# Shared expert's later quarters placed between the routed experts, three experts rounded early instead of five, one ring of four result tiles

## The chip, the cores and the metric

One Trainium2 chip, all 8 cores. Each core takes one of the 8 sequences (batch element b on core b) and runs the same program with the same weights; the cores exchange nothing. The time of a run is the device time of the slowest core in microseconds. A result is given as the median of several runs, and one execution more is taken with the hardware profiler.

## What is computed

One layer, for x of 8 x 2048 x 1024 in float32. First x plus an RWKV attention of the layer-normed x, then that plus a feed-forward part of its layer norm. Cut to what matters here:

```
xk, xv, xr = mixes of ln(x) with its shift by one token
k, v, r = xk@Wk.T, xv@Wv.T, xr@Wr.T ; wkv = recurrence over the 2048 tokens
x = x + (sigmoid(r) * wkv) @ Wo.T
f = ln(x)
combine = top-2 of 16 softmax router weights      # expert 15 is the identity
routed = combine[:, 15] * f + sum over e < 15 of combine[:, e] * ((silu(f@G[e]) * (f@U[e])) @ D[e])
shared = (silu(conv3(f)) * (f@Us)) @ Ds           # conv3: causal, kernel of 3 tokens, 1024 -> 512
x = x + shared + routed
```

## The kernel before

The text below calls TensorE PE, VectorE DVE, ScalarE ACT, GpSimd POOL and SyncE SP. Every engine has its own program in an order written out by hand, and they meet by counting semaphores. POOL issues all DMAs that convert float32 to bfloat16, that add in DRAM, or that go by an index; they run in the software queue q0. SP issues the plain ones, in the hardware queue q1. Both queues use the same 16 DMA engines.

**Attention** (to about 385 us). The tokens go in 4 chunks s of 512. For each chunk, 8 units d of 128 channels make k, v and r (24 matmuls) and the recurrence (`wkv` on DVE). In the chunk after it, `wo_tile` multiplies by the output weights, `x1add` adds to x (`x1r`, two buffers, loaded from x and stored to out by SP: tile g+2 is loaded after tile g has been stored), and `ln2` normalizes. From unit 7 on, POOL issues two `precast` DMAs for each unit: they turn the weights of the experts in `PRE` into bfloat16 in DRAM (`ewb_d`), a half matrix each, 30 in all, up to unit 21.

**Shared expert.** `gate_up(("S", c), ic)` makes a quarter ic of the 512 channels for chunk c: 24 matmuls for the convolution and 8 for `su`. `base(g)` multiplies a tile of 128 tokens by `sd` (8 matmuls); DVE copies the result to `fx[g % 4]`, and POOL adds it to out (`add_base`). A two-token halo is copied on DVE (`halo_s`). Chunks 0 and 1 stand among the router's work (`top2`, `ranks`, `route`). When the last tokens are routed, POOL scatters the table of positions, loads it as `ti`, and gathers rows.

**Routed experts** (from about 577 us). 15 experts, 320 rows each (3 tiles). For expert e PE does gate_up quarters 0 and 1, `down(e - 1)`, quarter 2, `rows_in(e + 1)` (transposes of the gathered rows) and quarter 3. ACT and DVE scale the results of `down` into `ysb` (a ring of 5 tiles), and POOL adds them to rows of out by index (`add_rows`). Adds of one expert are issued only when those of the expert before have landed, since two of them may touch the same row. ACT's and DVE's `yout(e - 1)` stand between silu and product of quarters 1 and 2 of expert e, and wait there for a free tile. Weights are 3 matrices of 1 MB (bfloat16) for each expert in 9 slots: from float32 by POOL (`expert_w`), or for experts of `PRE` from `ewb_d` by SP (`pre_w`), each when its slot is free (`w_free`). Weights 0 to 8 (experts 0 to 2) need not wait for an expert.

POOL's order in the loop of experts is:

```
rows(e + 2)
if e: add_rows(e - 1); expert_w(3 * e + 8)
if e == 1: add_rows(NE)        # the identity expert
expert_w(3 * e + 9), expert_w(3 * e + 10)
```

Of the kernel before, what the change touches and what calls it, by code (L numbers as in the profile page):

```python
# [30 lines left out]
PRE = [3, 5, 7, 9, 11]  # L31
NPOS = 128 * NPC

# [14 lines left out]
def build_one(ms, rec):  # L48
# [93 lines left out]
    wsl += [place(f"wsl{6 + j}", [128, 4096], BF16, o_m1 + 8192 * j)[0] for j in range(3)]  # L142
# [7 lines left out]
    xgT = [place(f"xgT{j}", [128, CC, CAP], BF16, o_x1 + 5120 * j)[0] for j in range(3)]  # L150
# [4 lines left out]
    xrow = [place(f"xrow{j}", [128, C], BF16, (o_y + 8192 if j < 4 else o_lt - 8192) + 2048 * j)[0] for j in range(8)]  # L155
    lnS = [place(f"lnS{j}", [128, CC, 528], BF16, o)[0] for j, o in enumerate((o_x, o_t))]
    sg = [place(f"sg{j}", [128, 512], F32, o_t + 8448 + 2048 * j)[0] for j in range(2)]
    ysb = [place(f"ysb{j}", [128, C], F32, o_m0 + 4096 * j)[0] for j in range(5)]
    idr = [place(f"idr{j}", [128, C], BF16, o_x + 2048 * j)[0] for j in range(TT)]
    hE = [place(f"hE{j}", [128, ICC, CAP], BF16, o)[0] for j, o in enumerate((o_m0 + 20480, o_x + 8448))]  # L160
    fx = [place(f"fx{j}", [128, C], F32, o_b + 4096 * j)[0] for j in range(4)]
# [23 lines left out]
    with ExitStack() as st:  # L185
# [12 lines left out]
        s_xrow = [sem(f"s_xrow{i}") for i in range(8)]  # L198
# [6 lines left out]
        s_acc = [sem(f"s_acc{i}") for i in range(2)]  # L205
# [6 lines left out]
        blocks = [("S", q) for q in range(NCH)] + [("E", e) for e in range(NE)]  # L212
        gu = {}
        for b in blocks:
            for ic in range(ICC):
                gu[(b, ic)] = len(gu)

        order = [0, NE] + list(range(1, NE))

        def ytile(e, j):  # L220
            return order.index(e) * TT + j
# [4 lines left out]
        def w_free(m):  # L226

            p = m - 9
            if p % 3 == 2:
                return MS(f"t:d{ytile(p // 3, TT - 1)}_1")  # L230
            return MS(f"t:{'gu'[p % 3]}{gu[(('E', p // 3), ICC - 1)]}")

        def ysb_free(eng, q):
            if q >= 5:
                k = (q - 5) // TT
                eng.wait_ge(s_acc[k % 2], 16 * TT * (k // 2 + 1))
# [40 lines left out]
        def _(t):  # L277
# [117 lines left out]
            def rows_in(e):  # L395
                for j, (o, w) in enumerate(TOKTILES):
                    n = column(e, j)
                    t.wait_ge(s_xrow[n % 8], 16 * (n // 8 + 1))
# [6 lines left out]
                    for kc in range(CC):  # L405
                        mm = t.transpose(xgps(n)[:, kc, 0:w], xrow[n % 8][0:w, 128 * kc:128 * (kc + 1)], IDM[0:w, 0:w])  # L406
# [7 lines left out]
            def gate_up(b, ic):  # L414
# [10 lines left out]
                if kind == "S":  # L425
# [5 lines left out]
                    for kk in range(3):  # L431
                        for kc in range(CC):
                            mm = t.matmul(ps[:, pg, :], cwS[:, kk * CC + kc, osl],  # L433
                                          lnS[q % 2][:, kc, 14 + kk:526 + kk],
                                          start=(kk == 0 and kc == 0), stop=(kk == 2 and kc == CC - 1))
# [3 lines left out]
                    for kc in range(CC):  # L439
                        mm = t.matmul(ps[:, pu, :], suS[:, kc, osl], lnS[q % 2][:, kc, 16:528],  # L440
                                      start=(kc == 0), stop=(kc == CC - 1))
                    PE(mm, f"u{n}")
                else:
# [3 lines left out]
                    for j, (bank, key) in enumerate(((pg, "g"), (pu, "u"))):  # L447
# [3 lines left out]
                        for kc in range(CC):  # L451
                            mm = t.matmul(ps[:, bank, 0:CAP], slot_view(m)[:, kc, osl], xgT[q % 3][:, kc, :],  # L452
# [3 lines left out]
            def down(e):  # L456
# [3 lines left out]
                for j, (o, w) in enumerate(TOKTILES):  # L460
                    q = ytile(e, j)
                    for h in range(2):
                        if q == 0:
                            t.wait_ge(s_dv, MS(f"v:fa{NT - 1}"))
                        else:
                            p = ytile(e, j - 1) if j else ytile(e - 1, TT - 1)
                            if h == 0:
                                t.wait_ge(s_sc, MS(f"s:y{p}"))
                            else:
                                t.wait_ge(s_dv, MS(f"v:yo{p}"))  # L470
# [4 lines left out]
                        PE(mm, f"d{q}_{h}")  # L475

            def base(g):
                c, i = g // 4, g % 4
                if g == 0:
                    t.wait_ge(s_sd, 16)  # L480
                    t.wait_ge(s_dv, MS("v:x1_15"))
                else:
                    t.wait_ge(s_dv, MS(f"v:fa{g - 1}"))
# [42 lines left out]
            for c in range(2, NCH):  # L526
                for ic in range(ICC):
                    gate_up(("S", c), ic)
                    base(4 * (c - 1) + ic)
            for g in range(12, 16):  # L530
                base(g)
            rows_in(0)
            for e in range(NE):
# [7 lines left out]
                gate_up(("E", e), 3)  # L541
            down(NE - 1)

        @blk.vector
        def _(v):
# [158 lines left out]
            def xg_out(e):  # L704
                for j, (o, w) in enumerate(TOKTILES):
                    n = column(e, j)
                    if n % 2 == 1:
                        v.wait_ge(s_pe, MS(f"t:xt{n}"))
                        if e >= 3:
                            v.wait_ge(s_pe, MS(f"t:u{gu[(('E', e - 3), ICC - 1)]}"))  # L710
                        DV(v.tensor_copy(xgT[e % 3][:, :, o:o + w], xgps(n)[:, :, 0:w]), f"xg{n}")
                DV.ms[f"v:xgt{e}"] = DV.v

            def hmul(b, ic):
# [9 lines left out]
                else:  # L724
                    if ic == 0 and q >= 2:
                        v.wait_ge(s_pe, MS(f"t:d{ytile(q - 2, TT - 1)}_1"))
                    DV(v.tensor_tensor(hE[q % 2][:, ic, :], sg[n % 2][:, 0:CAP], ps[:, pu, 0:CAP], OP.mult), f"h{n}")  # L727

            def yout(e):
                for j, (o, w) in enumerate(TOKTILES):  # L730
                    q, n = ytile(e, j), column(e, j)
                    wgt = tiw[0:w, n, 1:2]
                    ysb_free(v, q)
                    if e < NE:
                        v.wait_ge(s_pe, MS(f"t:d{q}_1"))
                        DV(v.tensor_scalar(ysb[q % 5][0:w, 512:1024], ps[0:w, 7, :], wgt, None, OP.mult), f"yo{q}")  # L736
                    else:
                        v.wait_ge(s_idr[j], 16)
                        DV(v.tensor_scalar(ysb[q % 5][0:w, 512:1024], idr[j][0:w, 512:1024], wgt, None, OP.mult),
                           f"yo{q}")  # L740

            def halo_s(q):
                v.wait_ge(s_pe, MS(f"t:u{gu[(('S', q - 1), ICC - 1)]}"))
                v.wait_ge(s_ls[(q - 1) % 2], 16 * ((q - 1) // 2 + 1))
                DV(v.tensor_copy(lnS[q % 2][:, :, 14:16], lnS[(q - 1) % 2][:, :, 526:528]), f"halo_s{q}")  # L745

            def base(g):
                v.wait_ge(s_pe, MS(f"t:f{g}"))
                if g >= 4:
                    v.wait_ge(s_out[g % 4], 16 * (g // 4))  # L750
                DV(v.tensor_copy(fx[g % 4][:], ps[:, 6:8, :].rearrange("p a b -> p (a b)")), f"fa{g}")
# [16 lines left out]
            for s in range(NCH):  # L768
                for d in range(CC):
# [12 lines left out]
                    if s == S_LAST and d == 0:  # L782
                        v.wait_ge(s_pe, MS("t:t1_15"))
                        DV(v.memset(lnS[0][:, :, 14:16], 0.0), "halo_s0")
# [3 lines left out]
            hmul(("S", 0), 0)  # L788
            x1add(12)
# [9 lines left out]
            halo_s(1)  # L799
            hmul(("S", 1), 0)  # L800
            base(0)
# [10 lines left out]
            for c in range(2, NCH):  # L812
                halo_s(c)
                for ic in range(ICC):
                    hmul(("S", c), ic)
                    base(4 * (c - 1) + ic)
            for g in range(12, 16):
                base(g)
            xg_out(0)
            for e in range(NE):  # L820
# [4 lines left out]
                if e == 1:  # L825
                    yout(NE)
# [3 lines left out]
                hmul(("E", e), 3)  # L830
            yout(NE - 1)

        @blk.scalar
        def _(s_):
# [85 lines left out]
            def xg_out(e):  # L920
                for j, (o, w) in enumerate(TOKTILES):
                    n = column(e, j)
                    if n % 2 == 0:
                        s_.wait_ge(s_pe, MS(f"t:xt{n}"))
                        if e >= 3:
                            s_.wait_ge(s_pe, MS(f"t:u{gu[(('E', e - 3), ICC - 1)]}"))
                        SC(s_.activation(xgT[e % 3][:, :, o:o + w], xgps(n)[:, :, 0:w], AF.Copy), f"xg{n}")  # L927
# [12 lines left out]
            def yout(e):  # L940
                for j, (o, w) in enumerate(TOKTILES):
                    q, n = ytile(e, j), column(e, j)
                    wgt = tiw[0:w, n, 1:2]
                    ysb_free(s_, q)
                    if e < NE:
                        s_.wait_ge(s_pe, MS(f"t:d{q}_0"))
                        SC(s_.activation(ysb[q % 5][0:w, 0:512], ps[0:w, 6, :], AF.Copy, scale=wgt), f"y{q}")  # L947
# [468 lines left out]
```

## Time and profile before

| what | value |
| --- | --- |
| median of 3 runs (lowest, highest) | 976.67 us (972.91, 987.81) |
| the profiled execution: its time | 965.69 us |
| its span on the slowest core (core 0) | 963.8 us |
| spans of the 8 cores | 930.8 to 963.8 us |
| PE, DVE, ACT, POOL busy, of the span | 70%, 42%, 33%, 22% |
| queue q0, queue q1, share of the 16 DMA engines | 66.7%, 18.8% |
| mean granted PE clock, core 0 | 0.876 of full speed |

The profile is of one execution, and its rows are of core 0. "Busy" of an engine is time in which it worked; the row of an instruction may name in brackets how long its engine stood idle before it and what ended that. The DMA share is the mean over the 16 DMA engines of the time that their packets took; in short stretches it can be a little over 1.

### The profile page before, as it was taken

Reading aid. Unit: us, or ns where it says so; the run is one execution under the profiler, and the core shown is the slowest. Engines: PE = TensorE matmul, PEld = TensorE weight load, DVE = VectorE, ACT = ScalarE, POOL = GpSimd, SP = SyncE. Lnnn points to the kernel's source line nnn. Section 1 sums busy time; section 2 is a strip of 40 time slices with the busy share of each in tenths; the row PEclk is TensorE's granted clock in tenths of the full one; section 3 lists DMA queues with packets and bytes.
Section 4 is the critical chain, followed back from the end, with each engine's and each line's share of the span. In section 5 each row is a group of like instructions: output and inputs, shape, how many; then the busy total and the mean of one; then the engine's idle time right before and its main releaser. Section 6 shows DMA issues by size and latency. Waiting matters only on the chain.

```text
span 963.8 us, 11603 instructions; the slowest of 8 cores (930.8 to 963.8 us)
## 1 busy us (share of the span) xinstructions
PE 671.9 (70%) x3677; PEld 340.5 (35%) x3732; DVE 401.2 (42%) x737; ACT 320.3 (33%) x560; POOL 214.2 (22%) x230
## 2 busy tenths in 40 slices
PE   1568568457684899976969968494929493984691
PEld 1133133123232444433434435253515251542350
DVE  5859966466576887430322132131202121221120
ACT  5295284326652547552200002121212121221120
POOL 2000111001000000054043034442415150641031
PEclk9989789779796999988979999797969797897895
DMA  6888699969996688823959969899999999999973
GB/s 149 166 156 148 82 138 162 144 135 129 165 133 164 127 233 176 244 97 58 188 114 173 162 118 217 170 197 210 203 206 183 241 177 228 174 177 177 179 122 57
DMA packets 40291, 156.11 MB, mean 162 GB/s; under 512 B 5792, under 2 KB 10016, under 8 KB 33568
## 3 DMA queue, kind: packets, MB, share of 16 engines
q0 software_dynamic: 23968, 101.79, 66.7%
q1 hardware_dynamic: 16256, 53.50, 18.8%
q8 instruction: 32, 0.52, 0.2%
q14 instruction: 35, 0.29, 0.1%
HBM read 169.27 MB, written 62.73 MB: 241 GB/s over the span
## 4 chain that ended last, share of the span: by engine, by line
DMA 35%; PE 34%; issue 10%; DVE 9%; ACT 8%; POOL 1%; another core or an unknown queue 0%; DVEq 0%; ACTq 0%; SPq 0%; POOLq 0%
DMA out<-ysb,ti 22%; PE ps L433 8%; PE ps L295 7%; PE ps L452 6%; DMA out<-x1r 6%; PE ps L472 4%; DMA x1r<-x 3%; DMA xr<-x 3%; PE ps L487 3%; PE ps L440 2%; PE ps L373 2%; DVE mix L579 1%; DVE mix L584 1%; POOL out L1078 1%; ACT ln1tok L851 1%
## 5 line engine op out<-in xcount | busy, mean ns | idle before, releaser
L295 PE MATMUL ps<-mix,wqkv 128*128 128x512 bf16 x748 | 191.0, 411 | 36.3 <-DVE mix L584 14.0
L452 PE MATMUL ps<-xgT,wsl 128*128 128x320 bf16 x960 | 149.9, 319 | 1.4 <-ACT xgT L927 1.4
L295 PEld LDWEIGHTS ps<-mix,wqkv 128*128 128x128 bf16 x768 | 78.9, 105 | 138.3 <-issue 65.7
L1078 POOL DMA_INDIRECT out<-ysb,ti x48 | 74.3, 1548 | 219.4 <-DVE ysb L736 150.8
L452 PEld LDWEIGHTS ps<-xgT,wsl 128*128 128x128 bf16 x960 | 97.6, 104 | 50.9 <-issue 7.2
L433 PE MATMUL ps<-lnS,cwS 128*128 128x512 bf16 x372 | 88.7, 392 | 17.2 <-DVE lnS L745 16.5
L406 PE MATMUL ps<-tri_sb,xrow 128*128 128x128 bf16 (+1 forms) x360 | 24.3, 220 | 106.1 <-ACT xgT L927 82.3
L736 DVE TENSOR_SCALAR ysb<-ps,ti 128x512 f32<-128x512 f32 (+1 forms) x45 | 33.7, 748 | 153.8 <-DMA out<-ysb,ti 106.2
L938 ACT ACTIVATE sg<-ps 128x320 f32<-128x320 f32 (+1 forms) x76 | 35.6, 469 | 179.1 <-PE ps L433 86.3
L472 PE MATMUL ps<-wsl,hE 128*128 128x512 bf16 (+1 forms) x345 | 85.0, 378 | 2.8 <-DVE hE L727 1.1
L947 ACT ACTIVATE ysb<-ps,ti 128x512 f32<-128x512 f32 (+1 forms) x45 | 30.9, 686 | 164.6 <-DMA out<-ysb,ti 114.1
L373 PE MATMUL ps<-wo_sb,yT 128*128 128x512 bf16 x252 | 60.5, 392 | 31.1 <-DVE x1r L628 27.0
L727 DVE TENSOR_TENSOR hE<-sg,ps 128x320 bf16<-128x320 f32 x60 | 29.3, 488 | 114.8 <-PE ps L452 103.3
L433 PEld LDWEIGHTS ps<-lnS,cwS 128*128 128x128 bf16 x384 | 38.3, 100 | 65.3 <-issue 23.5
L406 PEld LDWEIGHTS ps<-tri_sb,xrow 128*128 128x128 bf16 (+1 forms) x360 | 20.7, 102 | 110.9 <-issue 109.8
L1092 POOL DMA_DIRECT2D ewb_d<-ew x30 | 16.6, 552 | 180.0 <-PE ps L295 178.8
L723 DVE TENSOR_TENSOR hS<-sg,ps 128x512 bf16<-128x512 f32 x16 | 11.0, 688 | 100.8 <-PE ps L440 62.7
L472 PEld LDWEIGHTS ps<-wsl,hE 128*128 128x128 bf16 (+1 forms) x360 | 31.9, 100 | 53.7 <-issue 28.4
L1052 POOL DMA_INDIRECT xrow<-ln_d,ti x45 | 44.1, 980 | 20.6 <-issue 16.0
L373 PEld LDWEIGHTS ps<-wo_sb,yT 128*128 128x128 bf16 x256 | 25.4, 101 | 64.5 <-issue 37.7
L1042 POOL DMA_INDIRECT tab_d<-tok_sb,pidx x32 | 31.0, 967 | 65.9 <-DVE hS L723 35.5
L334 PE MATMUL ps<-tri_sb,ln1tok 128*128 128x128 bf16 x128 | 13.2, 266 | 43.4 <-ACT ln1tok L846 21.1
(130 smaller groups left out, 808.7 us busy)
## 6 DMA issues: line engine op xcount, KB each, us to landing
wsl<-ew POOLq DMA_DIRECT2D x30, 1024.0 KB, 21.2
ewb_d<-ew POOLq DMA_DIRECT2D x30, 512.0 KB, 21.3
wsl<-ewb_d SPq DMA_DIRECT2D x15, 1024.0 KB, 14.6
x1r<-x SPq DMA_DIRECT2D x18, 512.0 KB, 10.7
out<-x1r SPq DMA_DIRECT2D x16, 512.0 KB
out<-fx POOLq DMA_DIRECT2D x16, 512.0 KB, 7.3
xr<-x SPq DMA_DIRECT2D x14, 512.0 KB, 12.5
wqkv<-wq POOLq DMA_DIRECT2D x8, 768.0 KB, 8.9
```

Source lines behind the costliest of these rows:

```text
L295: mm = t.matmul(ps[:, 2 * b + n % 2, :], unit_w(d, b, kc), mix[s % 2][:, b, kc, :], start=(kc == 0), stop=(kc == CC - 1))
L373: mm = t.matmul(ps[:, 6 + h, :], yT[c % 2][:, kc, 128 * i:128 * (i + 1)], wo[:, kc, 512 * h:512 * (h + 1)], start=(kc == 0), stop=(kc == C ...
L406: mm = t.transpose(xgps(n)[:, kc, 0:w], xrow[n % 8][0:w, 128 * kc:128 * (kc + 1)], IDM[0:w, 0:w])
L433: mm = t.matmul(ps[:, pg, :], cwS[:, kk * CC + kc, osl], lnS[q % 2][:, kc, 14 + kk:526 + kk], start=(kk == 0 and kc == 0), stop=(kk == 2 a ...
L452: mm = t.matmul(ps[:, bank, 0:CAP], slot_view(m)[:, kc, osl], xgT[q % 3][:, kc, :], start=(kc == 0), stop=(kc == CC - 1))
L472: mm = t.matmul(ps[0:w, 6 + h, :], hE[e % 2][:, kc, o:o + w], slot_view(m)[:, kc, 512 * h:512 * (h + 1)], start=(kc == 0), stop=(kc == ICC ...
L736: DV(v.tensor_scalar(ysb[q % 5][0:w, 512:1024], ps[0:w, 7, :], wgt, None, OP.mult), f"yo{q}")
L938: SC(s_.activation(sg[n % 2][:, 0:w], ps[:, 2 * (n % 2), 0:w], AF.Silu), f"si{n}")
L947: SC(s_.activation(ysb[q % 5][0:w, 0:512], ps[0:w, 6, :], AF.Copy, scale=wgt), f"y{q}")
L1042: g_.indirect_dma_start(tab_d[:], bass.IndirectOffsetOnAxis(ap=pidx[:, c, g:g + 1], axis=0), tok[:, g, c, :], None).then_inc(s_scat, 16)
L1052: g_.indirect_dma_start(xrow[n % 8][0:w], None, ln2_d[:], bass.IndirectOffsetOnAxis(ap=ti[0:w, n, 0:1], axis=0)).then_inc(s_xrow[n % 8], 16)
L1078: g_.indirect_dma_start(out_d[:], bass.IndirectOffsetOnAxis(ap=ti[0:w, n, 0:1], axis=0), ysb[q % 5][0:w], None, compute_op=OP.add).then_in ...
```

## The change

- `PRE = [5, 8, 11]` instead of `[3, 5, 7, 9, 11]`. The DMAs that round early are quarters of a matrix instead of halves, still two for each unit, 36 in all, from unit 7 to unit 24.
- After `base(3)` PE does only quarters 0 and 1 of shared chunk 2, with `base(4)` and `base(5)`; then the experts begin. Of the six quarters that are left, one each stands behind experts 0, 2, 4, 6, 8 and 10, with one `base` each (6 to 11). `base(12)` and `base(13)` stand behind expert 11, 14 behind expert 12, 15 behind expert 13.
- `ysb` (5 tiles) and `fx` (4 tiles) become one ring `res` of 4 tiles, in the order `OUTS` in which results are made; tile r waits for the add of r - 4. Before the first add of a group (an expert's tiles, or base tiles in a row), POOL waits for every add of the group before (`added_before`).
- POOL's order in the loop changes, as below, and weights 5 to 8 and the first bases are issued directly behind `rows(0)`. The identity expert is added in iteration 8 instead of 1.
- `halo_s(1)` moves on DVE from behind `x1add(15)` to behind the first product of chunk 0, `halo_s(2)` from behind `route(1)`, `counts` and `base(3)` to behind the first product of chunk 1.
- `xrow` has 6 tiles instead of 8, `xgT` 2 instead of 3. Weight slot 8 lies where `ln2T` was, and `expert_w(8)` waits for that tile's last store. POOL waits for the last stores of `x1r` before `rows(0)`.

```diff
-PRE = [3, 5, 7, 9, 11]
+PRE = [5, 8, 11]
+FOLLOW = {0: (2, 2), 2: (2, 3), 4: (3, 0), 6: (3, 1), 8: (3, 2), 10: (3, 3)}
+LATE = {11: (12, 13), 12: (14,), 13: (15,)}
+IDE = 8
+def bases_after(e):
+    if e in FOLLOW:
+        c, ic = FOLLOW[e]
+        return (4 * (c - 1) + ic,)
+    return LATE.get(e, ())
+        def place_free(eng, r):
+            if r >= 4:
+                eng.wait_ge(s_out[r % 4], 16 * (r // 4))
+        def added_before(eng, r):
+            def group(k):
+                return OUTS[k][:2] if OUTS[k][0] == "E" else "B"
+            first = r
+            while first and group(first - 1) == group(r):
+                first -= 1
+            k = first - 1
+            while k >= 0 and group(k) == group(first - 1):
+                eng.wait_ge(s_out[k % 4], 16 * (k // 4 + 1))
+                k -= 1
...
 PE, the end of an iteration e (DVE and ACT alike)
                 gate_up(("E", e), 3)
+                if e in FOLLOW:
+                    c, ic = FOLLOW[e]
+                    gate_up(("S", c), ic)
+                for g in bases_after(e):
+                    base(g)
...
 POOL
-                i, j, h = u // 6, u // 2 % 3, slice(2048 * (u % 2), 2048 * (u % 2 + 1))
+                i, j, h = u // 12, u // 4 % 3, slice(1024 * (u % 4), 1024 * (u % 4 + 1))
...
-            for n in range(7, 7 + 3 * len(PRE)):
+            for n in range(7, 7 + 6 * len(PRE)):
...
             rows(0)
             g_.wait_ge(s_dv, MS("v:flag"))
-            for g in range(4, 12):
-                add_base(g)
-                if g in (4, 6, 8):
-                    expert_w((5, 6, 7)[g // 2 - 2])
-            identity_rows()
-            for g in range(12, 15):
-                add_base(g)
+            expert_w(5)
+            expert_w(6)
+            add_base(4)
+            expert_w(7)
             rows(1)
-            add_base(15)
+            add_base(5)
+            g_.wait_ge(s_lst[1], 16 * 2)
             expert_w(8)
             for e in range(NE):
-                if e + 2 < NE:
-                    rows(e + 2)
                 if e:
                     add_rows(e - 1)
                     if 3 * e + 8 < 3 * NE:
                         expert_w(3 * e + 8)
-                if e == 1:
+                if e == IDE:
                     add_rows(NE)
+                if e + 2 < NE:
+                    rows(e + 2)
                 for m in range(3 * e + 9, min(3 * e + 11, 3 * NE)):
                     expert_w(m)
+                for g in bases_after(e):
+                    add_base(g)
```

## Rows read from the trace of the kernel before

**Rows 1.** Waits, longest in total: engine, line, releaser: us, times, longest

```profile
ACT ysb L947 <- DMA out<-ysb,ti: 114.1, 8, 21.6
DVE x1r L628 <- DMA x1r<-x: 37.6, 4, 15.3
```

**Rows 2.** Stretches of core 0: busy by engine, PEclk, DMA share, GB/s

```profile
500.00:577.00 77.00, 68.40 (x316) 30.66 (x322) 18.58 (x20) 4.18 (x7) 19.42 (x23) 1.00 0.90 150
577.00:650.00 73.00, 53.45 (x380) 32.77 (x381) 18.55 (x32) 18.62 (x31) 31.73 (x29) 0.91 0.95 195
650.00:900.00 250.00, 169.68 (x1100) 100.17 (x1110) 49.14 (x84) 49.10 (x84) 83.87 (x75) 0.84 1.02 197
900.00:952.00 52.00, 31.88 (x182) 16.61 (x182) 10.09 (x16) 9.50 (x16) 13.62 (x9) 0.83 0.80 138
```

**Rows 3.** The same columns, short stretches whose DMA work is known

```profile
444.00:454.00 10.00, 5.42 (x22) 2.59 (x23) 1.36 (x2) 3.71 (x4) 1.83 (x3) 0.66 0.62 107
616.00:620.00 4.00, 0.00 (x0) 0.00 (x0) 1.27 (x3) 1.95 (x3) 1.21 (x1) 0.50 0.06 11
940.00:952.00 12.00, 2.30 (x10) 0.71 (x8) 1.49 (x2) 0.80 (x2) 4.54 (x3) 0.67 0.66 109
```

**Rows 4.** DMA view of 650:900: queue packets, MB, share; issues, us to landing

```profile
q0 software_dynamic: 8067, 37.48, 86.7%
q1 hardware_dynamic: 1578, 11.45, 14.8%
...
wsl<-ew POOLq DMA_DIRECT2D x18, 1024.0 KB, 30.8
...
out<-ysb,ti POOLq DMA_INDIRECT x30, 24.9
xrow<-ln_d,ti POOLq DMA_INDIRECT x27, 32.0
```

**Rows 5.** Timeline of PE, gate and up quarters of experts, one pair apart

```profile
620.60 8.01 PE L452 MATMUL ps<-xgT,wsl 128*128 128x320 bf16 x48
819.74 9.11 PE L452 MATMUL ps<-xgT,wsl 128*128 128x320 bf16 x48
858.17 8.37 PE L452 MATMUL ps<-xgT,wsl 128*128 128x320 bf16 x48
916.96 8.31 PE L452 MATMUL ps<-xgT,wsl 128*128 128x320 bf16 x48
```

**Rows 6.** Timeline of DVE: first unit of chunks 1, 2, 3; waits for x

```profile
115.67 0.69 DVE L608 TENSOR_TENSOR evb<-eb,ps 128x512 f32<-128x512 f32 x1
188.92 1.22 DVE L628 SCALAR_TENSOR_TENSOR x1r<-ps,x1r 128x1024 f32<-128x1024 f32 x1 [13.84 <-DMA x1r<-x]
...
222.07 0.69 DVE L608 TENSOR_TENSOR evb<-eb,ps 128x512 f32<-128x512 f32 x1
245.67 0.69 DVE L608 TENSOR_TENSOR evb<-eb,ps 128x512 f32<-128x512 f32 x1 [8.02 <-ACT eb L904]
297.42 1.23 DVE L628 SCALAR_TENSOR_TENSOR x1r<-ps,x1r 128x1024 f32<-128x1024 f32 x1 [15.34 <-DMA x1r<-x]
322.04 0.68 DVE L608 TENSOR_TENSOR evb<-eb,ps 128x512 f32<-128x512 f32 x1
```

**Rows 7.** Timeline of PE and POOL around the halo and the table

```profile
430.66 3.57 PE L433 MATMUL ps<-lnS,cwS 128*128 128x512 bf16 x8 [6.27 <-DVE lnS L745]
...
499.53 0.56 POOL L1087 DMA_DIRECT2D wsl<-ew  x1
...
618.79 1.56 POOL L1078 DMA_INDIRECT out<-ysb,ti  x1 [12.52 <-ACT ysb L950]
```

**Rows 8.** The DMA view of 116:222: queues, and issues with us to landing

```profile
q0 software_dynamic: 2158, 7.86, 61.9%
...
ewb_d<-ew POOLq DMA_DIRECT2D x16, 512.0 KB, 21.4
...
x1r<-x SPq DMA_DIRECT2D x4, 512.0 KB, 17.0
```

More of the change, by code:

```diff
@@ L30, with order_of_results @@
 SPARE_ROWS = 128 * TT
-PRE = [3, 5, 7, 9, 11]
+PRE = [5, 8, 11]
 NPOS = 128 * NPC
+FOLLOW = {0: (2, 2), 2: (2, 3), 4: (3, 0), 6: (3, 1), 8: (3, 2), 10: (3, 3)}
[6 more added lines that the diff above has]
+    return LATE.get(e, ())
+def order_of_results():
+    outs = [("B", g) for g in range(6)]
+    for e in range(NE):
+        if e:
+            outs += [("E", e - 1, j) for j in range(TT)]
+        if e == IDE:
+            outs += [("E", NE, j) for j in range(TT)]
+        outs += [("B", g) for g in bases_after(e)]
+    return outs + [("E", NE - 1, j) for j in range(TT)]
+OUTS = order_of_results()
 class Done:
@@ L141, in build_one @@
     wsl = [place(f"wsl{j}", [128, 4096], BF16, o_a + 8192 * j)[0] for j in range(6)]
-    wsl += [place(f"wsl{6 + j}", [128, 4096], BF16, o_m1 + 8192 * j)[0] for j in range(3)]
+    wsl += [place(f"wsl{6 + j}", [128, 4096], BF16, o_m1 + 8192 * j)[0] for j in range(2)]
+    wsl += [place("wsl8", [128, 4096], BF16, o_l2)[0]]
     o_r = o_a + 8192 * 5
@@ L149, in build_one @@
     rkf, _ = place("rkf", [128, 16, NT], F32, o_r + 6912)
-    xgT = [place(f"xgT{j}", [128, CC, CAP], BF16, o_x1 + 5120 * j)[0] for j in range(3)]
+    xgT = [place(f"xgT{j}", [128, CC, CAP], BF16, o_x1 + 5120 * j)[0] for j in range(2)]
     cwS, _ = place("cwS", [128, 24, I], BF16, o_m0)
@@ L197, in build_one @@
         s_pre = [sem(f"s_pre{i}") for i in range(len(PRE))]
-        s_xrow = [sem(f"s_xrow{i}") for i in range(8)]
+        s_xrow = [sem(f"s_xrow{i}") for i in range(6)]
         s_idr = [sem(f"s_idr{i}") for i in range(TT)]
@@ L209, in build_one @@
         PE, DV, SC = Done(s_pe, ms, "t"), Done(s_dv, ms, "v"), Done(s_sc, ms, "s")
[L212 to L221, printed above, removed]
+        quarters = [(("S", c), ic) for c in range(2) for ic in range(ICC)] + [(("S", 2), 0), (("S", 2), 1)]
+        for e in range(NE):
+            quarters += [(("E", e), ic) for ic in range(ICC)]
+            if e in FOLLOW:
+                quarters += [(("S", FOLLOW[e][0]), FOLLOW[e][1])]
+        gu = {q: n for n, q in enumerate(quarters)}
         def column(e, j):
@@ L525, in _ @@
             base(3)
[L526 to L531, printed above, removed]
+            gate_up(("S", 2), 0)
+            base(4)
+            gate_up(("S", 2), 1)
+            base(5)
             rows_in(0)
@@ L788, in _ @@
             hmul(("S", 0), 0)
+            halo_s(1)
             x1add(12)
@@ L798, in _ @@
             x1add(15)
-            halo_s(1)
             hmul(("S", 1), 0)
+            halo_s(2)
             base(0)
@@ L811, in _ @@
             base(3)
[L812 to L818, printed above, removed]
+            hmul(("S", 2), 0)
+            halo_s(3)
+            base(4)
+            hmul(("S", 2), 1)
+            base(5)
             xg_out(0)
@@ L830, in _ @@
                 hmul(("E", e), 3)
+                if e in FOLLOW:
+                    c, ic = FOLLOW[e]
+                    hmul(("S", c), ic)
+                for g in bases_after(e):
+                    base(g)
             yout(NE - 1)
@@ L1018, in _ @@
             silu(("S", 1), 3)
-            for c in range(2, NCH):
-                for ic in range(ICC):
-                    silu(("S", c), ic)
+            silu(("S", 2), 0)
+            silu(("S", 2), 1)
             xg_out(0)
@@ L1033, in _ @@
                 silu(("E", e), 3)
+                if e in FOLLOW:
+                    c, ic = FOLLOW[e]
+                    silu(("S", c), ic)
             yout(NE - 1)
```

157 lines of the change are left out of this document (80 added, 77 removed).

## The prediction

> **What bounds the kernel now.** I read the list of waits first. The longest that cost anything are ACT's in the expert stage, for adds into out, 114 us in 8 waits; the same list shows DVE waiting 38 us for loads of x in the attention [rows 1]. Then the stretches. From 500 to 577 us (the shared expert) PE works 68.4 of 77 us; from 577 to 900 (experts) 223.1 of 323 us, so it idles 100 us. The DMA share there is 0.95, then 1.02 over 250 us: the 16 engines never rest [rows 2]. So the adds are late because they stand in q0 behind weights, and the expert stage is bound by the DMA engines, not by the ring in which the results wait. I test that with prices.
>
> A weight of 1.05 MB converted from float32, alone in its stretch: 0.62 x 10 us = **6.2 us** of all 16 engines. Three adds of one expert, alone at the end: 0.66 x 12 = **7.9 us**, so 3.1 us for a whole base tile of 0.52 MB (the three carry 1.31 MB) [rows 3]. A weight from `ewb_d`: q1 takes 14.8% of 250 us, 37 us for 11.45 MB, so **3.4 us**. q0 takes 86.7% of it, 217 us, for 18 weights (112), 30 adds (79) and 27 gathers, which leaves 26 us or 1 us for each [rows 4]. An expert with converted weights then costs 18.6 + 7.9 + 2.9 = 29.4 us, one rounded early 10.2 + 7.9 + 2.9 = 21.0, and a pair 50.4. PE's timeline has four such pairs in 199.1 us (49.8 each) and the last two intervals, both of converted experts, in 58.8 us (29.4 each) [rows 5]. PE's own work for an expert is 17 us (223.1 us over the 13 experts of that time) [rows 2]. The DMA model holds within 2%.
>
> **The change part by part**, against the profiled execution's 965.7 us (the median of the runs shown, 976.67, is 1.0114 times that).
>
> *Six shared quarters and ten bases leave the front.* The stretch from 500 to 577 us has 316 matmuls in 68.4 us, 0.216 us each, so a quarter with its base (32 + 8 matmuls) takes PE 8.7 us; six of them and four bases more make about 60 us that enter 100 us of idle. Experts start some 60 us earlier. On PE that is worth 60 us; on the DMA engines, nothing: the ten adds of base tiles (31 us of engines) move with them, and every weight, add and gather still has to pass. What can be won is only DMA idle. After the table is loaded (weight 4 is issued at 499.5 [rows 7]) this is 0.10 x 77 = 7.7, 0.05 x 73 = 3.7 and, in the tail to 952, 0.20 x 52 = 10.4: 22 us [rows 2].
>
> *Two experts more are converted in the loop.* 2 x 3 x (6.2 - 3.4) = **+17 us**, all on the bound. If the two queues together run better than alone it is nearer 12; the two intervals in rows 5 give 29.4 - 20.4 = 9 for an expert, 18.
>
> *Base adds stand between the groups, and each waits.* `add_base` now waits on POOL until the adds of the expert before have landed, and the next `add_rows` until the base tile has. Queued behind this second wait are, on POOL, the adds, weight 3e + 8 of the next iteration, its gathers and two weights. While POOL stands at it, q0 holds only what is ahead of the base tile, and as that is the last entry, its landing means an empty queue. At 616 to 620 us the trace has one such spot (the identity expert's adds behind expert 0's): share 0.06, so 3.8 us of nothing, then adds issued at 618.8 [rows 3, 7]. I take 4 us. It comes with base 6, 7, 8, 9, 10, 11 and with 12 and 13 together: 7 x 4 = 28 us. The tail becomes a chain: adds of 11, weight 44, base 14, adds of 12, base 15, adds of 13, of 14. The work in it is 4 x 7.9 + 6.2 + 2 x 3.1 = 44 us. Of its six hand-overs weight 44 covers one and PE's last expert shares in another; for the rest I take 3 to 4 us each, 14 idle. Idle in all 42 instead of 22: **+20 us**. Bounds: 0 for a drain (an early-rounded weight in q1 fills it; 9 are left) gives -8; 5.5 for a drain gives +30.
>
> The Trainium skill (DMA: Bandwidth & Descriptors, section on the anatomy of one DMA, SWDGE path) puts the fixed cost around a DMA at about 2.0 us, mostly the write's receipt. By that figure seven drains cost 14 us and not 28. The trace's stretch at 616 us speaks for nearly twice as much, with POOL's issue in it, so the row is used.
>
> *Early rounding at half the rate.* In the chunks of attention with `precast`, two DMAs of 0.52 MB per unit keep q0 at 61.9%, and a load of `x1r` takes 17 us to land; SP's chain of store, load, store, load passes through that queueing several times in each chunk [rows 8]. DVE waits 13.8 us for one and 15.3 for another, and the unit that starts at 245.7 waited 8.0 for its layer norm's x [rows 6]. Chunk 1 takes 222.1 - 115.7 = 106.4 us, chunk 2 takes 100.0. Without waits I count 9 us for each of four units and 12 for each of the four with output tiles, 84 us. So at most 22 + 16 = 38 us plus what ln1 gives, some 45 in all. The change halves the bytes that each unit issues, so in chunk 1 q0's 7.86 MB become about 4. The queue is no longer full, and I take three quarters of the 45: **-33 us**. The lower bound is 10 (the chain still has store before load), the upper 45. It moves everything behind it, weight 4 and the table too. That rounding now ends at unit 24 puts `su` and the first `cw` two units later on POOL; they are needed after unit 31, so nothing.
>
> *Halos.* PE waits 6.3 us for `halo_s(1)`, which on DVE stands behind `x1add(15)` [rows 7]. It moves ahead, and this part of PE's order leads to `ranks(1)` and the table: **-6 us** (0 if a table load or the next layer norm is late instead). `halo_s(2)` frees PE 9 us later on, but POOL's table is later than that: 0.
>
> *The rest.* The ring of four: tile r waits for r - 4, that is an add of the expert before, where the old ring let two tiles go on the one before that. ACT and DVE stand at it, and behind them silu and transposes. It is covered by the same 100 us of PE idle (now 40); with the DMA bound it costs nothing unless PE's late quarter 3 holds back `w_free`: 0, up to +8. The gathers of e + 2 stand behind the adds and one weight on POOL; they still land within the iteration: 0, up to +5. Fewer `xrow` and `xgT` tiles, no row against it: 0.
>
> **Sum:** -33 - 6 + 17 + 20 = -2, so 964 for the profiled execution and 964 x 1.0114 = **975 us**.
>
> **The rivals.** *A, faster: the drains are cheap.* If q1's weights or spare packets fill them (2 us each, 14 in all) and the attention gives its full 45: -45 - 6 + 17 + (14 + 14 - 22) = -28, or 948 us. For it: all cores' x loads are late, and the ends of one group may overlap the issue of the next. Against it: the stretch at 616. *B, slower: the attention hardly gains.* The place is SP's chain of store then load of `x1r`. If half the traffic still makes a load land after 15 us, DVE's two long waits stay; the attention gives 10 and the ring holds PE back for 5: -10 - 6 + 17 + 20 + 5 = +26, or 1003 us. It decides from a landing time of about 13 us upwards; for it speaks that a load has two stores ahead of it in any case; against it, that the queue goes from full to about two thirds. *C: PE's idle was the ring's fault, and filling it shortens the stage by the full 60:* -60 - 33 + 17 = -76, 900 us. The share of 1.02 and the sum of prices speak against it.
>
> **How the numbers follow.** Forecast 0.47, A 0.26, B 0.20, C 0.05, something else 0.02. A change of 2% is about what a measurement of this kernel tells from none, so within 957 to 996 is "same". Faster: A's share of 0.24, C, and a little of the forecast: 0.31. Slower: B and some of the forecast's upper edge: 0.24. Same: 0.45. The forecast's own range is 955 to 993 (drains 2 to 5.5 us, attention -25 to -40); with A's and B's centres and their bounds, 940 to 1010.
>
> **What would show it.** The DMA share near 1 from the table to 880 us but for some seven gaps of 4 us, each behind a base tile's add. Weight 4 issued near 460. Landing of x loads in chunks 1 and 2 under 10 us, and no wait over 5 us of DVE for x. PE still idle a fifth of the expert stage. A converted pair of experts at 63 to 66 us. The prediction is wrong if the gaps are missing, if the attention ends later than 365, or if experts pass faster than their 29.4 us of DMA.

## The result and the profile after

| | before | after |
| --- | --- | --- |
| median, lowest to highest | 976.83 us, 965.5 to 999.41 (14 runs) | 988.83 us, 977.39 to 996.38 (14 runs) |
| profiled execution: time, span | 965.69, 963.8 us | 978.70, 977.3 us |

The ratio is 1.0111, with a 95% interval of 1.0062 to 1.0159: slower by about 1%, inside the 2% that were called "same", but clear of zero and on the other side of the forecast (975 us, 0.2% less). Ratios, here and below, leave disturbed executions out, so they need not be the quotient of the medians.

The page of the changed kernel, on its slowest core (core 7; that of before was core 0). Parts 1, 3 and 4:

```profile
PE 714.2 (73%) x3732; PEld 352.2 (36%) x3732; DVE 402.1 (41%) x737; ACT 322.0 (33%) x560; POOL 219.6 (22%) x242
...
q0 software_dynamic: 25696, 101.79, 65.9%
q1 hardware_dynamic: 15392, 47.21, 15.8%
...
DMA xrow<-ln_d,ti 11%; DMA out<-res 9%; DMA out<-res,ti 8%; PE ps L503 8%; PE ps L346 7%; PE ps L484 5%; PE ps L424 5%; PE ps L516 5%; DMA x1r<-x 4%; DVE mix L630 2%; DVE mix L625 2%; PE ps L491 1%; PE ps L530 1%; DMA tab_d<-tok_sb,pidx 1%; ACT ln1tok L902 1%
```

The same part of the page of before begins:

```profile
DMA out<-ysb,ti 22%; PE ps L433 8%; PE ps L295 7%; PE ps L452 6%; DMA out<-x1r 6%; PE ps L472 4%; DMA x1r<-x 3%; DMA xr<-x 3%; PE ps L487 3%; PE ps L440 2%; PE ps L373 2%; DVE mix L579 1%; DVE mix L584 1%; POOL out L1078 1%; ACT ln1tok L851 1%
```

Before, the adds of experts headed the chain with 22%; they (`out<-res,ti`) are down to 8%. In front now stand two things that were not in the list: loads of gathered rows (`xrow`) with 11%, and adds of base tiles (`out<-res`) with 9%.

The waits of core 7, with those that answer to [rows 1] (engine, line, releaser: us in total, times, longest):

```profile
PE ps L457 <- DMA xrow<-ln_d,ti: 64.9, 19, 14.7
...
POOL out L1146 <- DMA out<-res,ti: 51.2, 4, 30.1
POOL out L1124 <- DMA out<-res: 42.3, 3, 25.0
ACT res L998 <- DMA out<-res: 37.5, 2, 24.8
...
ACT res L998 <- DMA out<-res,ti: 32.3, 7, 9.8
PE ps L516 <- ACT res L998: 32.2, 7, 11.3
...
DVE x1r L674 <- DMA x1r<-x: 13.3, 3, 7.1
```

DVE's wait for x has fallen from 37.6 to 13.3 us. But now POOL waits at the base adds for the expert adds (51 us) and at the expert adds for the base adds (42 us), which is what `added_before` asks for, and PE waits 65 us for gathered rows.

Stretches, columns as in [rows 2] and [rows 3]; the second row is of core 0 of before, the others are of core 7 of the changed kernel:

```profile
461.40:955.70 494.30, 336.70 (x1952) 185.89 (x1952) 94.77 (x147) 82.51 (x137) 151.39 (x141) 0.82 0.91 163
499.00:944.10 445.10, 324.41 (x1976) 180.64 (x1996) 96.95 (x151) 81.40 (x138) 148.23 (x136) 0.88 0.96 182
528.00:532.00 4.00, 3.13 (x39) 2.45 (x37) 1.79 (x3) 1.46 (x2) 0.91 (x1) 1.00 0.02 4
592.00:596.00 4.00, 3.72 (x23) 2.16 (x21) 0.69 (x1) 1.01 (x2) 0.00 (x0) 0.50 0.33 115
596.00:600.00 4.00, 4.00 (x28) 2.75 (x27) 0.86 (x2) 0.46 (x2) 3.18 (x2) 0.90 0.44 50
660.00:664.00 4.00, 0.00 (x0) 0.00 (x0) 0.00 (x0) 0.00 (x0) 0.00 (x0) 0.50 0.38 136
664.00:668.00 4.00, 2.79 (x7) 1.05 (x8) 0.75 (x1) 0.69 (x1) 2.44 (x2) 0.50 0.56 16
664.00:667.00 3.00, 1.78 (x5) 0.72 (x6) 0.75 (x1) 0.69 (x1) 1.63 (x1) 0.50 0.00 0
848.00:852.00 4.00, 0.84 (x3) 0.32 (x4) 1.23 (x1) 0.00 (x0) 1.62 (x1) 0.50 0.06 11
892.00:896.00 4.00, 4.00 (x22) 2.30 (x20) 0.42 (x1) 0.44 (x1) 2.99 (x2) 0.50 0.31 31
```

The first two rows are the whole way from the load of the table to the issue of the last add: DMA share 0.91, where the same way before has 0.96. The others are five of the predicted gaps, each behind a base tile's add (issued at 519.6, 583.9, 633.3, 824.5 and 863.6 us). One of them on POOL's timeline (start, duration, idle before):

```profile
618.58 1.22 POOL L1133 DMA_DIRECT2D wsl<-ew  x2
633.31 0.91 POOL L1146 DMA_DIRECT2D out<-res  x1 [13.51 <-issue]
665.29 1.63 POOL L1124 DMA_INDIRECT out<-res,ti  x1 [31.07 <-DVE res L782]
667.20 1.57 POOL L1124 DMA_INDIRECT out<-res,ti  x1 [0.27 <-PE ps L516]
669.03 1.42 POOL L1124 DMA_INDIRECT out<-res,ti  x1 [0.27 <-PE ps L516]
669.95 1.14 POOL L1133 DMA_DIRECT2D wsl<-ew  x1
671.36 1.03 POOL L1103 DMA_INDIRECT xrow<-ln_d,ti  x1 [0.27 <-issue]
...
695.20 0.60 POOL L1133 DMA_DIRECT2D wsl<-ew  x1 [8.64 <-PE ps L503]
```

and the timelines of PE and of ACT beside it:

```profile
652.02 1.89 PE L516 MATMUL ps<-wsl,hE 128*128 128x512 bf16 x8
665.22 3.50 PE L516 MATMUL ps<-wsl,hE 128*128 128x512 bf16 x8 [11.31 <-ACT res L998]
...
677.46 2.97 PE L503 MATMUL ps<-xgT,wsl 128*128 128x320 bf16 x16
688.62 1.01 PE L457 MATMUL ps<-tri_sb,xrow 128*128 128x128 bf16 x8 [8.19 <-DMA xrow<-ln_d,ti]
...
664.38 0.69 ACT L998 ACTIVATE res<-ps,ti 128x512 f32<-128x512 f32 x1 [12.70 <-DMA out<-res]
```

The base tile's add is issued at 633.3, the last entry of q0. It lands just before 664.4, since ACT, which waits for the same tile, goes on there. By then the queue has run dry: from 664 to 667 us the share is 0.00. POOL issues the next add at 665.3, then more adds, a weight and the gathers, in this order. The gathered rows reach PE at 688.6, so quarter 3 ends late, the slots come free late, and POOL issues the next weight at 695.2.

### The profile page after: what moved, and what is told of

The parts are those of the page before. It is cut to its first block, busy times and chain, and to the rows that moved or that the text cites. A ratio compares the mean times of both kernels' runs of the same rounds, so it can differ in the third digit from the quotient of the medians.

```text
span 977.3 us, 11740 instructions; the slowest of 8 cores (949.4 to 977.3 us)
## 1 busy us (share of the span) xinstructions
PE 714.2 (73%) x3732; PEld 352.2 (36%) x3732; DVE 402.1 (41%) x737; ACT 322.0 (33%) x560; POOL 219.6 (22%) x242
## 4 chain that ended last, share of the span: by engine, by line
DMA 35%; PE 33%; issue 10%; DVE 8%; ACT 8%; POOL 3%; ACTq 0%; DVEq 0%; POOLq 0%; SPq 0%
DMA xrow<-ln_d,ti 11%; DMA out<-res 9%; DMA out<-res,ti 8%; PE ps L503 8%; PE ps L346 7%; PE ps L484 5%; PE ps L424 5%; PE ps L516 5%; DMA x1r<-x 4%; DVE mix L630 2%; DVE mix L625 2%; PE ps L491 1%; PE ps L530 1%; DMA tab_d<-tok_sb,pidx 1%; ACT ln1tok L902 1%
## 5 line engine op out<-in xcount | busy, mean ns | idle before, releaser
L346 PE MATMUL ps<-mix,wqkv 128*128 128x512 bf16 x768 | 208.3, 435 | 30.7 <-DVE mix L630 13.5
L503 PE MATMUL ps<-xgT,wsl 128*128 128x320 bf16 x960 | 155.7, 325 | 1.1 <-ACT xgT L978 1.1
L516 PE MATMUL ps<-wsl,hE 128*128 128x512 bf16 (+1 forms) x360 | 94.0, 400 | 33.8 <-ACT res L998 32.2
L1124 POOL DMA_INDIRECT out<-res,ti x48 | 74.0, 1541 | 188.2 <-DVE res L782 55.9
L457 PE MATMUL ps<-tri_sb,xrow 128*128 128x128 bf16 (+1 forms) x360 | 31.7, 252 | 109.0 <-DMA xrow<-ln_d,ti 64.9
L782 DVE TENSOR_SCALAR res<-ps,ti 128x512 f32<-128x512 f32 (+1 forms) x45 | 33.6, 748 | 118.4 <-PE ps L516 59.7
L424 PE MATMUL ps<-wo_sb,yT 128*128 128x512 bf16 x256 | 70.3, 437 | 6.5 <-ACT lnT L942 3.5
L998 ACT ACTIVATE res<-ps,ti 128x512 f32<-128x512 f32 (+1 forms) x45 | 30.9, 686 | 121.7 <-PE ps L516 51.9
L457 PEld LDWEIGHTS ps<-tri_sb,xrow 128*128 128x128 bf16 (+1 forms) x360 | 25.5, 117 | 117.3 <-issue 116.6
L1138 POOL DMA_DIRECT2D ewb_d<-ew x36 | 18.8, 523 | 191.4 <-PE ps L346 184.0
L978 ACT ACTIVATE xgT<-ps 128x1024 bf16<-128x1024 bf16 (+1 forms) x23 | 20.1, 875 | 87.7 <-PE ps L457 87.7
## 6 DMA issues: line engine op xcount, KB each, us to landing
out<-res POOLq DMA_DIRECT2D x16, 512.0 KB, 16.4
```

The lines of the kernel that those rows point to most:

```text
L346: mm = t.matmul(ps[:, 2 * b + n % 2, :], unit_w(d, b, kc), mix[s % 2][:, b, kc, :], start=(kc == 0), stop=(kc == CC - 1))
L424: mm = t.matmul(ps[:, 6 + h, :], yT[c % 2][:, kc, 128 * i:128 * (i + 1)], wo[:, kc, 512 * h:512 * (h + 1)], start=(kc == 0), stop=(kc == C ...
L457: mm = t.transpose(xgps(n)[:, kc, 0:w], xrow[n % 6][0:w, 128 * kc:128 * (kc + 1)], IDM[0:w, 0:w])
L516: mm = t.matmul(ps[0:w, 6 + h, :], hE[e % 2][:, kc, o:o + w], slot_view(m)[:, kc, 512 * h:512 * (h + 1)], start=(kc == 0), stop=(kc == ICC ...
L782: DV(v.tensor_scalar(res[r % 4][0:w, 512:1024], ps[0:w, 7, :], wgt, None, OP.mult), f"yo{n}")
L998: SC(s_.activation(res[r % 4][0:w, 0:512], ps[0:w, 6, :], AF.Copy, scale=wgt), f"y{n}")
```

## The account

To compare kernels I use five numbers for each core: the end of the attention (start of the last unit's first exp), the issue of the table's load, the first expert's matmul, the issue of the last add, and the DMA share between table and last add. Share times length is "busy", the rest "idle". The last column is what PE waits for gathered rows. Means over the 8 cores of each profiled execution; the kernels below `after` are those of the experiments:

```
kernel            attention  table  first expert  last add   way   busy  idle  PE waits for xrow
before              367.8    484.6     568.8       928.1    443.4  421.3  22.2    10.1
after               339.8    458.4     477.9       945.0    486.7  444.6  42.1    63.6
e1_rows_first       339.6    457.9     477.4       929.4    471.5  440.8  30.7    24.6
e3_weight_behind    337.0    454.2     473.5       918.8    464.6  439.6  25.0    57.3
e13_both            337.2    454.9     474.3       913.2    458.4  441.7  16.6    27.2
e2_base_aside       337.2    454.9     474.3       903.7    448.9  442.1   6.8    43.9
b_pre               335.6    453.7     537.7       910.1    456.4  441.6  14.9    27.6
a_pre               366.2    483.1     502.3       945.6    462.5  419.7  42.8    52.5
b_halo              368.1    484.6     557.2       918.2    433.6  424.3   9.3     8.0
c1_pre_halo         338.8    459.0     531.4       910.5    451.6  448.2   3.4    27.9
e13_again           337.2    455.9     476.4       923.4    467.4  451.1  16.4    28.4
```

How far these numbers carry: a share is given to 0.01, so the idle time of one core is good to some 2 us. `e13_both` and `e13_again` are one kernel on two chips; idle agrees (16.6 and 16.4), but busy is 441.7 and 451.1. So a few us of busy between two kernels show little.

After against before: the table 26 us earlier, busy +23, idle +20, so the last add 17 us later on the mean of the cores (on the slowest 944.1 to 955.7, 11.6 us). The slowest core is not the same one in both, so the mean and the maximum need not move alike.

## The experiments

The theory at this point (T1): the mutual wait of base adds and expert adds empties q0. Its rivals: T2, the gathers behind the adds are late; T3, the two experts more that are converted make the loss. Four kernels, built from the changed kernel, tell them apart. They were timed on one chip, each against the kernel before; the changed kernel was not timed there, so its 1.0111 is from another set of runs.

**Gathers first.**

```diff
             for e in range(NE):
+                if e + 2 < NE:
+                    rows(e + 2)
                 if e:
                     add_rows(e - 1)
...
-                if e + 2 < NE:
-                    rows(e + 2)
```

> The changed kernel with one step of POOL's loop put back where it was: rows(e + 2) is issued at the start of iteration e, ahead of add_rows(e - 1). The changed kernel stands at 1.011 of the kernel before. Theory T2 (the gathers stand behind the adds of an expert and a weight, so PE waits for them, and with quarter 3 the weight slots come free late): PE's waits for xrow, 65 us on core 7 of the changed kernel, fall under 20 us, and the time falls by 15 to 30 us, to a ratio of 0.98 to 0.995. Theory T1 (q0 runs empty behind every base tile's add, since POOL waits for it before it issues the next adds): the gathers are now issued at that spot and cover some 3 us of each of seven gaps, but in the same order the rest stays; 5 to 15 us, ratio 0.995 to 1.006. Theory T3 (the two experts more that are converted fill the DMA engines): nothing, 1.011.

Ratio 0.9878 (0.9723 to 1.0034), 23 us less than the changed kernel's 1.0111; in the profiles the last add comes 16 us earlier. In the account the wait for xrow falls from 64 to 25 us, and the idle time from 42 to 31 us (28 to 34 on every core). The time and the waits are what T2 said, the idle time is within what T1 said; this kernel alone does not tell the two apart. PE's gain is not all kept: its waits behind ACT for a tile of `res` rise from 26 to 44 us on the mean of the cores.

**Base tiles aside.**

```diff
+    sh_d = dram("sh_d", [T, C], F32, "Internal")
...
 added_before
+            if OUTS[r][0] == "B" and OUTS[r][1] >= 6:
+                return
             k = first - 1
-            while k >= 0 and group(k) == group(first - 1):
+            while OUTS[k][0] == "B" and OUTS[k][1] >= 6:
+                k -= 1
+            last = k
+            while k >= 0 and group(k) == group(last):
...
 add_base
+                dst = sh_d if g >= 6 else out_d
```

> The changed kernel in which the base tiles 6 to 15 are added into a DRAM tensor of their own instead of into out (so that part of the sum is left out of the result), and no add waits for them nor they for any; the number and size of all DMAs stay. T1: the gaps behind the base adds go, 25 to 40 us off the changed kernel's time, ratio 0.97 to 0.985. T2: the waits for xrow stay above 45 us and the time falls by 10 us at most, 1.00. T3: no change, 1.011.

Ratio 0.9685 (0.9581 to 0.9789), the fastest of all, at the lower end of what T1 said (0.97 to 0.985) or a little beyond; it leaves the base tiles 6 to 15 out of the result. Idle is 6.8 us. Two stretches of its core 0, columns as above:

```profile
465.50:922.00 456.50, 322.98 (x1980) 179.93 (x1978) 95.78 (x148) 82.97 (x138) 151.30 (x141) 0.86 0.97 177
486.00:900.00 414.00, 296.38 (x1835) 166.93 (x1836) 86.73 (x135) 75.50 (x127) 129.52 (x120) 0.86 0.99 182
```

and waits of the same core, PE's for gathered rows and ACT's for a tile whose base add has not landed:

```profile
PE ps L463 <- DMA xrow<-ln_d,ti: 45.3, 7, 13.0
...
ACT res L1004 <- DMA sh_d<-res: 34.1, 2, 20.1
```

From 486 to 900 us the engines are full at 0.99 although PE waits 45 us for late gathers. So in this kernel late gathers cost nothing by themselves: they are hidden as long as q0 holds other work. In the changed kernel they come on top of a queue that has just been emptied. T2 then is no second cause beside T1, but what T1 makes of an order that is harmless here. The second line settles a rival that the theories leave out, the ring of four: ACT waits as long for the slots of base tiles as on this core of the changed kernel (34.1 us against 35.6), and the idle time is gone all the same. It is POOL's wait that empties the queue.

**A weight behind the base adds.**

```diff
-                for m in range(3 * e + 9, min(3 * e + 11, 3 * NE)):
-                    expert_w(m)
+                if 3 * e + 9 < 3 * NE:
+                    expert_w(3 * e + 9)
                 for g in bases_after(e):
                     add_base(g)
+                if 3 * e + 10 < 3 * NE:
+                    expert_w(3 * e + 10)
```

> The changed kernel with POOL's last step of an iteration swapped: weight 3e + 9, then the base adds, then weight 3e + 10, so that q0 holds 6 us of work when the base tile lands. T1: five of the seven gaps close (two of the six stand where the weights come from SP), 12 to 25 us less, ratio 0.985 to 1.00. T2: 0 to 5 us. T3: nothing.

Median 959.63 us (954.92 to 988.47, 4 runs) beside 973.84 for the kernel before on that chip. The ratio is 0.986, from two runs (954.92 and 956.95 us) and a mean of 969.4 us for the kernel before, too few for an interval. Idle falls by 17 us to 25, while PE still waits 57 us for gathered rows. It is T1's expectation, at its better end: a swap of two lines turns a loss of 1% into a gain of about 1.4%.

**Both edits.**

> Both of the last: gathers first, and weight 3e + 10 behind the base adds. If T1 and T2 each hold and add up, 30 to 45 us off the changed kernel's time and the ratio is 0.965 to 0.98, faster than both kernels; if one of them is only the other's shadow, no better than the better of the two single edits. T3: 1.00 to 1.011.

Median 953.69 us (949.23 to 964.89, 4 runs). The ratio is 0.979, from two runs (mean 949.5 us) and the same 969.4, again without an interval. Idle 16.6 us. Against the changed kernel 25 us of idle are gone, where the single edits took 11 and 17: nearly additive. The time moved only 6 us beyond the better one, to the upper end of the expected 0.965 to 0.98. Timed again, beside the last kernel below:

> The changed kernel with gathers first and weight 3e + 10 behind the base adds, timed again on one chip with the last: ratio 0.97 to 0.985, idle of the DMA engines on the way near 17 us on the mean of the cores.

Ratio 0.9840 (0.9763 to 0.9918), idle 16.4 us. As expected.

**The early rounding alone, in the kernel before**, and **the old rounding in the changed kernel**. The edit of the first; the second is its reverse:

```diff
-PRE = [3, 5, 7, 9, 11]
+PRE = [5, 8, 11]
...
-                i, j, h = u // 6, u // 2 % 3, slice(2048 * (u % 2), 2048 * (u % 2 + 1))
+                i, j, h = u // 12, u // 4 % 3, slice(1024 * (u % 4), 1024 * (u % 4 + 1))
...
-            for n in range(7, 7 + 3 * len(PRE)):
+            for n in range(7, 7 + 6 * len(PRE)):
...
-                sy.wait_ge(s_pre[i], 16 * 6)
+                sy.wait_ge(s_pre[i], 16 * 12)
```

> The kernel before with one part of the change alone: PRE = [5, 8, 11], rounded in 36 quarters instead of 30 halves. The prediction's terms say -33 us for the attention and +17 us for two experts more that are converted between the experts, together -16, ratio 0.983: the load of the table should be issued some 33 us earlier and the way from there to the last add be 17 us longer. From the changed kernel's trace the attention term looks like -26 to -29 (the last unit's exp starts at 330 to 347 us instead of 361 to 376). If the conversion costs nothing where the DMA engines are full anyway, the way from the table to the end stays at 443 us and the ratio is 0.97; if T3 holds (conversion is the changed kernel's whole loss) it grows by 40 us and the ratio is above 1.01.

Ratio 0.9868 (0.9820 to 0.9917); predicted 0.983. Table 31 us earlier, the attention 32, busy +20, idle -7, so the way is 13 us longer where 17 were expected. Why idle time falls is open.

> The changed kernel with the old early rounding, PRE = [3, 5, 7, 9, 11] in 30 halves. By the prediction's terms it loses the attention's gain and gains the 17 us back: ratio 1.011 + 0.016 = 1.027. If the conversion costs nothing on the way from the table to the end (T1, T2: that way is long because q0 runs empty and gathers come late), it is 1.035 to 1.045, and that way stays near 487 us. T3: it is 440 to 450 us, and the ratio 0.99.

Ratio 1.0207 (1.0048 to 1.0366); predicted 1.027. Table 25 us later than in the changed kernel, busy -25, idle the same (42.8 against 42.1). T3 is out: with the old conversions the way still has all of its idle time, and the kernel is not faster (T3 said 0.99, outside the interval).

How a load of `x1r` fares in the changed kernel's chunk 1, from the DMA view of 116:222 on core 7, which answers to [rows 8]:

```profile
q0 software_dynamic: 2643, 4.82, 41.3%
...
ewb_d<-ew POOLq DMA_DIRECT2D x20, 256.0 KB, 8.8
x1r<-x SPq DMA_DIRECT2D x6, 512.0 KB, 10.8
xr<-x SPq DMA_DIRECT2D x5, 512.0 KB, 7.7
```

q0's share falls from 61.9% to 41.3%, and a load lands after 10.8 us instead of 17.0 (the median of each).

**The halo copies alone, in the kernel before.**

```diff
             def halo_s(q):
-                v.wait_ge(s_pe, MS(f"t:u{gu[(('S', q - 1), ICC - 1)]}"))
+                if q >= 2:
+                    v.wait_ge(s_pe, MS(f"t:u{gu[(('S', q - 2), ICC - 1)]}"))
...
             hmul(("S", 0), 0)
+            halo_s(1)
             x1add(12)
...
-            halo_s(1)
             hmul(("S", 1), 0)
+            halo_s(2)
...
             for c in range(2, NCH):
-                halo_s(c)
                 for ic in range(ICC):
                     hmul(("S", c), ic)
+                    if c == 2 and ic == 0:
+                        halo_s(3)
```

> The kernel before with the halo copies alone moved as in the change (halo_s(1) behind the first product of chunk 0, halo_s(2) and halo_s(3) likewise ahead). The prediction's term is -6 us at the load of the table, since PE's wait of 6.3 us ahead of shared chunk 1 goes. PE's wait of 8.6 us ahead of chunk 2 goes as well and, as the expert stage of this kernel starts behind PE, not behind the table, that may add up: 6 to 15 us at the first expert. What arrives at the end depends on the DMA engines, 0 to 10 us: ratio 0.99 to 1.00.

Ratio 0.9864 (0.9793 to 0.9936), a little more than the expected 0 to 10 us. But not where the prediction had it: on the mean of the cores the table stays at 484.6. What moves is the first expert, 12 us earlier, and with it the idle time of the engines, 22 to 9 us.

The mean hides that the cores fall into two halves. In every profiled execution here the four cores of one half need 13 to 19 us longer from the end of the attention to the table than those of the other: before, cores 0 to 3 need 125.3 us on the mean and cores 4 to 7 108.4; in this kernel, whose late half is cores 4 to 7, it is 125.4 and 107.6. So the halos moved the table by 0 to 1 us in either half. Nearly all cores of the late half have waits there that the profile puts down to "remote", something outside the core's own rows; the other half has none. What they are is open.

The trace of before shows why 6.3 us was a poor price. On core 5, two waits between 400 and 500 us:

```profile
PE ps L433 <- DMA lnS<-l2t_d: 18.8, 1, 18.8
PE ps L433 <- DVE lnS L745: 1.9, 1, 1.9
```

and on core 0, the one that was read, between 400 and 450 us:

```profile
ACT L938 <- remote: 13.7, 1, 13.7
...
PE ps L433 <- DVE lnS L745: 6.3, 1, 6.3
DVE x1r L628 <- remote: 4.7, 1, 4.7
```

On core 0, 4.7 of the 6.3 us at the first halo were `x1add(15)` waiting for something outside the core's own rows; on core 5 the wait is 1.9 us. `x1add(15)` also stands ahead of the layer norm and the routing of the last tokens, so the table needs it wherever the halo copy is; that this is why nothing arrives is argued from the order of the code.

Ahead of chunk 2 the halves differ as well. PE's timeline of core 0, then SP and PE of core 5:

```profile
489.63 7.10 PE L433 MATMUL ps<-lnS,cwS 128*128 128x512 bf16 x23 [8.57 <-DVE lnS L745]
...
443.62 26.50 SPq L1214 DMA_DIRECT2D lnS<-l2t_d  x2
...
480.32 7.38 PE L433 MATMUL ps<-lnS,cwS 128*128 128x512 bf16 x24 [18.83 <-DMA lnS<-l2t_d]
```

Core 0 waits 8.6 us for the second halo, and with the copies moved this wait is gone. Core 5 waits 18.8 us for chunk 2's load, which was issued at 443.6 and took 36.5 us to land; in this kernel no load of `lnS` takes over 27 us on any core, and PE waits at most 7 us for one. Why they land sooner is not shown. The three halo copies were moved together, so the gain is not divided among them.

**The two parts together, with the old order of the experts.** The edits are those of `b_pre` and `b_halo`.

> The kernel before with the two parts of the change that do not touch the order of the experts: PRE = [5, 8, 11] in quarters and the halo copies moved. Alone they gave 0.987 and 0.986. The account by the way from the table to the last add (mean over the cores: 443 us before, 456 with the new PRE, 434 with the halos) says that they add up: table at 453, way 447, ratio 0.970 to 0.977. If the shared quarters between the experts are worth something of their own (PE's 60 us in idle time), this kernel must be slower than the repaired order of the changed kernel (0.979 in its first timing); if the stage is bound by the DMA engines, as the prediction has it, it is as fast or faster.

Ratio 0.9764 (0.9689 to 0.9839), idle 3.4 us. The two gains of 0.987 and 0.986 multiply to 0.973, which lies within the interval. The table comes at 459.0, 6 us later than expected, and the way is 451.6 where 447 was expected. The kernel has none of the shared quarters between the experts and is not slower than the repaired order (0.984, intervals overlapping; medians 954.18 and 964.91 us on the same chip). Its ratio is the lowest of the kernels that compute the whole.

## Why the prediction was wrong, step by step

- **The bound.** Right. Six quarters and ten bases moved into PE's idle time bring nothing of their own: PE starts the experts 91 us earlier (568.8 to 477.9), 26 of them from the table and 65 from the move (predicted about 60), and the last add comes 17 us later. c1 against e13 says the same with few gaps.
- **Two experts more converted, +17 us.** Right in kind; the size came out as +17 to +25. Busy rises by 25 us from a_pre to after and by 20 from before to b_pre, but by 17 from b_halo to b_pre, which ran on one chip and differ otherwise in the halos alone. One kernel on two chips differs by 9, so that this term was too small is not shown.
- **Idle of the engines, 22 to 42 us, +20.** Measured 22.2 to 42.1. The number is right partly by luck. The mutual wait is the cause (6.8 us remain without it), but **the step "the gathers of e + 2 ... still land within the iteration: 0, up to +5" failed**: PE's waits for them went from 10 to 64 us, and with the gathers put back first idle is 31 us instead of 42, so they were worth 11 us of it. The seven gaps of 4 us and the tail of 14 were priced too high by about as much as the gathers were priced too low. The lone gap at 616 us [rows 3] had a whole queue ready to be issued behind it; those of the changed kernel have PE waiting as well.
- **Attention, -33 us.** Measured -28 on the mean of the cores between before and after (-32 in b_pre). Right within its bounds; DVE's wait for x falls from 39 to 16 us. Its signs came only in part: loads of x land after 10.8 us in chunk 1 and 14.1 in chunk 2, not under 10, and DVE's longest wait for one is 7.1 us, not under 5. Rival B, with its turn at 13 us, did not come.
- **Halos, -6 us. This step failed**: nothing arrives at the table (108.4 to 107.6 us behind the attention in the early half of the cores, 125.3 to 125.4 in the late one). The row was read on the slowest core alone. That core is of the late half, and its wait is three times that of core 5.
- **`halo_s(2)`: 0.** Not isolated in the changed kernel, where the experts start 19 us behind the table. In the old order, where PE's chain of shared chunks leads to the first expert, the copies together brought 1.4%.
- **Ring of four: 0.** Right as far as it was tested. In e2 the ring is the same, PE still waits 20 us on the mean of the cores for its tiles (26 in the changed kernel), and the engines are full.

Summed on the mean of the cores: predicted -39 at the table, +17 and +20 behind it, together -2; measured -26, +23, +20, together +17. In front 13 us are missing: 6 of the halos, 5 of the attention, and 2 of the stretch between them. Behind, 6 us of busy are too many, of which see above. So the forecast fell on the wrong side through the halos, which gave nothing, through an attention gain 5 us smaller than priced, and through busy time. The gathers, which it set at nothing without a row, cost 11 us of idle time; in the sum the drains, priced too high, hid them. Of the 17 us 12 reach the slowest core.

PE's idle time was also misjudged: from the first expert to the last add core 7 has PE busy for 334 of 475 us, so it idles 30%, not a fifth.

Open is why cores 4 to 7 need 494 to 501 us for the way in the changed kernel and cores 0 to 3 only 471 to 480; they differ in busy (448 to 454 us against 436 to 441) as well as in idle. The data differ, and so do the times at which the cores reach the stage (446 to 461 us for cores 4 to 7, 455 to 470 for the others); nothing was tried to part the two.

## What to carry to other kernels

When the DMA engines are the bound, price a new wait of the issuing engine by what is left in its queue when the wait ends: a wait behind a DMA that is the last entry empties the queue, and one more transfer issued behind that DMA (here one weight, two lines) covers a part of it: 17 of 42 us here. Work moved under a DMA-bound stage gained nothing here; look for what the move frees ahead of the stage, or leave the order alone. Read a wait on several cores before it becomes a term: the same wait was 6.3 us on the slowest core and 1.9 us on another.

## What the runs showed of the hardware

The granted clock is 0.50 (1.2 GHz) from 660 to 664 us, where PE stands still, and still 0.50 from 592 to 596, where it has work again. Matmuls behind an idle stretch are slow: 48 matmuls of gate and up take 9.12 us behind one, at a mean clock of 0.73, and 6.69 at a clock of 1.00. Two rows of core 7 of the changed kernel:

```profile
532.13 6.69 PE L503 MATMUL ps<-xgT,wsl 128*128 128x320 bf16 x48
...
643.07 9.12 PE L503 MATMUL ps<-xgT,wsl 128*128 128x320 bf16 x48
```

So this stall cost PE 2.4 us more than its own length. PE idles 30% of the stage, so little should depend on it; no run tests that.

A weight that is converted on its way costs the engines 6.2 us alone. Among others, by the differences above (17 to 25 us for six weights), it costs 2.8 to 4.1 us more than one that is already bfloat16 (3.4 us).
